# Six unread matmuls on TensorE between the mixing and the first projection of a transformer layer

## The reference, cut to what matters

```
h = tok(x, ...)                       # a state-space kernel: for 256 channels, a sum over 64 poles of complex powers
h = h + attn(layernorm(h), w_q, w_k, w_v, w_o)   # 16 heads, 4 key/value heads, head size 128, rotary, causal
h = h + ffn(layernorm(h), ...)        # 8 experts chosen by a gate, rank-8 updates
```

## Time and profile before

| | us |
|---|---|
| median of 3 runs | 862.8 (862.48 to 863.54) |
| the profiled execution's own time | 863.28 |
| its span, first to last instruction | 861.5 |
| TensorE busy in it | 766.9 (89%) |
| VectorE, ScalarE, GpSimd busy | 594.4, 457.3, 449.8 |
| mean granted TensorE clock | 0.969 |

### The profile page before, as it was taken

How to read it: one execution, slowest core, us unless ns; L and a number is a source line. 1 busy time by engine, 2 the same in 40 slices (tenths; PEclk the granted TensorE clock), 3 DMA queues, 4 the chain that set the end, 5 groups by cost and what they waited for, 6 DMA issues and landing times.

```text
span 861.5 us, 17620 instructions
## 1 busy us (share of the span) xinstructions
PE 766.9 (89%) x5880; PEld 706.6 (82%) x5880; DVE 594.4 (69%) x1618; ACT 457.3 (53%) x1243; POOL 449.8 (52%) x669
## 2 busy tenths in 40 slices
PE   0059975889999999999999999999999999999985
PEld 0058875779999999999999999999999998998762
DVE  7958983767776666566656565666565777777877
ACT  6324432656666565656656565655656555545421
POOL 0196761555454574644457474444565655656513
PEclk9999986889999999999999999999999999999996
DMA  9004335010001010200001020000010000000001
GB/s 201 0 1 70 62 63 220 25 37 2 0 0 37 1 51 2 74 0 0 0 1 50 1 75 0 0 0 0 2 49 2 1 2 25 24 24 24 1 25 73
DMA packets 31043, 26.43 MB, mean 31 GB/s; under 512 B 22988, under 2 KB 23372, under 8 KB 30740
## 3 DMA queue, kind: packets, MB, share of 16 engines
q1 hardware_dynamic: 30996, 25.84, 11.2%
HBM read 17.44 MB, written 8.39 MB: 30 GB/s over the span
## 4 chain that ended last, share of the span: by engine, by line
PE 77%; DVE 11%; POOL 6%; issue 3%; ACT 2%; DMA 1%; SPq 0%; DVEq 0%; POOLq 0%; ACTq 0%
PE bank L1176 17%; PE bank L1178 17%; PE bank L1177 17%; PE bank_pair L1176 4%; PE bank_pair L1178 4%; PE bank_pair L1177 4%; PE bank L1189 3%; POOL w_lo L422 2%; PE bank L1298 2%; PE bank_pair L1298 2%; PE bank_pair L1308 1%; PE bank L1308 1%; PE bank L1312 1%; PE bank L1252 1%; DVE bank_pair L864 1%
## 5 line engine op out<-in xcount | busy, mean ns | idle before, releaser
L1176 PE MATMUL bank<-xt_hi,w_hi 128*128 (+1 forms) x768 | 218.0, 284 | 2.3 <-DVE xt_lo L937 1.5
L1178 PE MATMUL bank<-xt_lo,w_hi 128*128 (+1 forms) x768 | 215.7, 281 | 0.0
L1177 PE MATMUL bank<-xt_hi,w_lo 128*128 (+1 forms) x768 | 215.6, 281 | 0.0
L945 DVE TENSOR_TENSOR kq<-bank,cst 128x512 f32<-128x512 f32 (+1 forms) x96 | 57.8, 603 | 143.6 <-ACT swap L659 107.3
L490 POOL TENSOR_TENSOR swap<-swap,cst 128x512 f32<-128x512 f32 (+1 forms) x96 | 105.7, 1103 | 84.4 <-ACT swap L659 80.5
L1176 PEld LDWEIGHTS bank<-xt_hi,w_hi 128*128 128x128 f32 x768 | 145.7, 190 | 3.3 <-issue 1.9
L1178 PEld LDWEIGHTS bank<-xt_lo,w_hi 128*128 128x128 f32 x768 | 145.5, 190 | 0.0
L1177 PEld LDWEIGHTS bank<-xt_hi,w_lo 128*128 128x128 f32 x768 | 145.4, 189 | 0.0
L347 POOL TENSOR_TENSOR spare<-cst 1x1 f32<-1x1 f32 x87 | 16.6, 191 | 230.8 <-DVE rinv L1079 141.2
L699 ACT ACTIVATE sm<-sm,mx 128x128 f32<-128x128 f32 (+1 forms) x256 | 113.6, 445 | 21.9 <-DVE mx L1069 21.8
L658 ACT ACTIVATE swap<-bank 64x512 f32<-64x512 f32 (+1 forms) x96 | 50.2, 523 | 127.8 <-PE bank L1178 125.1
(11 more groups left out here) (241 smaller groups left out, 1904.3 us busy)
## 6 DMA issues: line engine op xcount, KB each, us to landing
mixed<-st SPq DMA_DIRECT2D x64, 64.0 KB, 2.2
out<-x SPq DMA_DIRECT2D x16, 256.0 KB, 2.0
raw<-in_w_qkv SPq DMA_DIRECT2D x8, 384.0 KB, 3.7
raw<-in_w_o SPq DMA_DIRECT2D x10, 256.0 KB, 2.7
x<-mixed SPq DMA_DIRECT2D x2, 1280.0 KB, 10.9
norm_mem<-in_w_qkv SPq DMA_DIRECT2D x6, 384.0 KB, 3.8
x<-mixed SPq DMA_DIRECT2D x3, 512.0 KB, 4.5
norm_mem<-in_w_o SPq DMA_DIRECT2D x6, 256.0 KB, 2.8
```

Of the source, the lines that this page charges most:

```text
L945: v.tensor_tensor(view(kq), src, table(cosT), ALU.mult).then_inc(kq_cos, 1)
L1176: mmul(dst, lh, rh, start=start and k == 0, stop=False, skip_group_check=True)
L1177: mmul(dst, ll, rh, start=False, stop=False, skip_group_check=True)
L1178: last = mmul(dst, lh, rl, start=False, stop=stop and k == n - 1, skip_group_check=True)
```

## The change

TensorE gets six more matmuls, each the 128x128 identity against the first 512 columns of the table of constants, into bank 0 of PSUM, where nobody reads them: five after the product of line 1208, behind a wait until ScalarE has copied the last mixed chunk, and one between the transposes of token row 0 and the wait for `xt_lo`. The projection's first matmul starts bank 0 anew.

```
             last.then_inc(cw_mm, 1)
 
+            def keep_warm(count):
+
+                for _ in range(count):
+                    mmul(banks[0][:], ident, cst[:, 0:512], start=True, stop=True)
+
+            pe.wait_ge(evac, NQ)
+            keep_warm(5)
+
...
             first_tokens(0)
+            keep_warm(1)
             wait_split(pe, KC - 1)
             pe.wait_ge(xt_lo, 2)
             project(0, 0, True, lambda: None, lambda: first_tokens(1))
```

## The result

The changed kernel's median is 861.24 us over 20 runs (858.75 to 863.13), against 863.4 us for the kernel before over 20 runs beside it (861.96 to 864.59). The ratio is 0.9974, with a 95% interval of 0.9965 to 0.9982: 2.2 us faster, between 1.6 and 3.0. Both kernels spread by 2.5 us and more from run to run, more than the change moves them, so a single execution proves little about the time. Its trace shows the mechanism all the same.

The account below looks back on a forecast made before the run. TensorE's low clock from 124.80 to 145.28 us slows the projection on the chain of waits. An earlier rise gains 3.5 x 0.5 = 1.7 us, less 0.2: from the median 862.8 to 861.3 us, range 859.8 to 863.1.

Parts of the forecast that it names:

- The five cost nothing: After line 1208's product, the five matmuls lie beside the load of token row 0: 0 us, at most 1.0.
- rival D: Before the projection: the five hold up the transposes, 1.5 us slower, time 864.3; chance 0.05.
- low-level price of 1.84 us: One float32 matmul of 512 columns in a row at the low clock takes 1.84 us, 0.92 at the full level.
- The five gain nothing: Before token row 0's transposes: the five raise the clock, but most is lost again by 136.88 or shortly after.
- rival A: The clock stays up from the five until the projection; transposes and projection run full: gain 2.9 us, time 859.9; chance 0.14.
- The single matmul does it: Filling the hole before the projection brings the rise to 141.8: 1.7 us gained, less 0.2 for a later start.
- Rival B: Before the projection: transposes do not help raise the clock; gain 0.6 us, time 862.2; chance 0.24.
- The fall at 841.6: Near the end the clock fell with little idle time after mostly transposes, taken as a sign that transposes don't count.
- Rival C: Products with the mostly zero identity leave the clock as it was; only 0.2 us cost is left, time 863.0; chance 0.07.
- The pauses behind: After the projection, the pauses before the scores and later move as a whole, unchanged, and do not take the gain.

Follow-up runs that it names:

- the two in one hole: The change with two unread matmuls instead of one in the 1.5 us hole before the projection; 861.34 us, 0.9979 of the kernel before.
- the second trace of the change: The change itself, unaltered, run again as the base for other kernels; 861.5 us, 0.9976 of the kernel before.
- the transposes' trace: Each of the change's six unread matmuls replaced by eight 128x128 transposes of the constants; 861.36 us, 0.9973 of the kernel before.

## Why the prediction was right, and where not

**The time** was forecast at 861.3 and came at 861.24, but that agreement is partly luck: the gain was forecast at 1.5 us and measured at 2.2 (1.6 to 3.0), and the runs of before that I started from had a median 0.6 us under that of the twenty. I had given 0.40 to a gain of over 0.2%, and 0.57 to less; 0.26% was measured.

**The five cost nothing**: right. They ended at 132.9, within the 132.8 to 134.2 of the forecast; rival D's delay appeared nowhere. The low-level price of 1.84 us is borne out by the two in one hole (3.62 us).

**The five gain nothing**: right in the median, shown by the kernel with the five alone (0.9995) and by the one without them (0.9972). The step under it was only half right. I had said that the clock is lost 2.2 to 2.4 us after TensorE stops. It fell 3.7 us after the five in the changed kernel's trace, 2.9 to 3.1 us after them in the traces of the six other kernels with five (or forty transposes) and a pause of over 4 us, and not at all over 2.95 us in the second trace of the change. Two falls were too few to price rival A by. So rival A is part of the truth for some executions.

**The single matmul does it**: right, shown by the kernel that has it alone. Its gain is the term that I sized too small, at 1.5 us. I put the rise 4.9 us after the transposes' start. In the seven traces in which the hole was filled and the clock was down at the transposes it came 2.7, 3.1 and five times 5.4 to 5.6 us after it: 4.7 in the mean, near the forecast, though none of the seven lies near it. Two things were put at nothing in the sum: executions in which the clock is never down, and the pause behind the scores, below. When it comes early, the whole 5.0 us of low clock in the projection are gone, 5.0 x 0.44 = 2.2, less 0.33 for the later start: 1.9, as measured at the scores. When it comes late, it is 0.9 at the scores (the transposes' trace); when it was never down, 2.8. The four traces of kernels with the hole filled by one matmul or its eight transposes, at most five ahead of it and the pauses behind left alone give 28.18, 28.87, 29.07 and 30.09, mean 29.05; the two with the hole open give 30.97 and 31.32, mean 31.15: 2.1 us, near the measured 2.2. At the attention product the same six traces give 49.08 and 51.54: 2.5 us. Six traces are few, so both are estimates of the mixture and not its proof.

**Rival B** fell with the transposes that raised the clock. The fall at 841.6 that spoke for it is left without a cause: no run was made for it, and the one filler behind those transposes in the last kernels was not tried alone. **Rival C** fell with the change's own trace: the identity's matmuls raised it.

**The pauses behind**: the forecast said that they would stay as they were. In the change's trace they did; the clock fell again at 153.6 and at 174.1, and the step between took 20.3 us as before. In the transposes' trace the low stretch behind the scores was half as long, and 1.0 us more was gained there. That filling the first of them would gain nothing I had not seen: VectorE's longer addition and GpSimd take it.

**Open**: whether two in the hole lose what the sum says, and how often in many executions the clock stays up until the projection; the runs do not settle either. Why VectorE's addition in line 951 takes 2.70 us with the first pause filled and 1.49 without was not tried.

## What to carry to other kernels

Look for the hole just ahead of dense work, and not for the long pause before it: here one unread matmul in 1.5 us of standing gave what six gave, and five in a pause of 9 us gave nothing. Price a higher clock only as far as TensorE stays on the chain of waits: 5.0 us of low clock in the projection cost 2.2 us, but filling the pause ahead of 5.7 us of it in the first attention step gained nothing, because the chain went over to GpSimd and VectorE. Where a run varies with the moment at which the clock changes, take two traces of the same kernel before believing one.

## What the runs showed of the hardware

Float32 transposes raise and hold TensorE's clock as matmuls do: behind 1.9 us of matmuls, 40 of them ran from 127.73 to 133.05, with the rise at 129.3 and 1.00 after it. Products whose weights are the identity do so too: in the second trace of the change they ran from 127.67, and the rise came among them at 131.7.

In the pauses ahead of the product of line 1208 and behind the five the fall came between 2.2 and 4.1 us after TensorE had stopped; at 4.1 us, in the trace of the one alone, TensorE had already been working again for 1.1 us. Behind the last product of the kernel with nine and all pauses filled it came after 1.4 us (851.46 to 852.84). The length of the pause alone does not decide it: the clock stayed up over 2.95 us in the second trace of the change and fell 2.94 us after the five in the kernel with five and all pauses filled. The rise came between 2.7 and 6.1 us after unbroken work began.

The change thus gives 858.5 to 863.1 us over 31 runs, while the two kernels in which nine matmuls close the pause and the second pause and the end are filled too stay within 856.9 and 858.6 us over ten runs (one of them leaves out the first pause). That the varying moment of the rise makes the spread is likely and not shown: the kernel before spreads by 2.6 us as well.
